# GpSimd's share of the square roots: one cubic step per piece, and 60 pieces in place of 16

## The reference

```
d2   = maximum(q2[..., :, None] + k2[..., None, :] - 2.0 * qk, 1e-12)
attn = softmax(-sqrt(d2), axis=-1)
out  = einsum('bhij,bhjd->bhid', attn, v)
```

## Time and profile before

| | us |
|---|---|
| median of 3 runs | 1478.41 |
| lowest and highest | 1476.91, 1479.61 |
| span of the profiled execution (the page gives no other time of it) | 1475.7 |
| ScalarE busy | 1445.4 |
| VectorE busy | 1245.1 |
| TensorE busy | 1125.2 |
| GpSimd busy | 632.5 |
| ScalarE's chain, share of the span | 72% |

### The profile page before, as it was taken

How to read it: one execution, slowest core, us unless ns; L and a number is a source line. 1 busy time by engine, 2 the same in 40 slices (tenths; PEclk the granted TensorE clock), 3 DMA queues, 4 the chain that set the end, 5 groups by cost and what they waited for, 6 DMA issues and landing times.

```text
span 1475.7 us, 21637 instructions
## 1 busy us (share of the span) xinstructions
PE 1125.2 (76%) x7910; PEld 441.5 (30%) x7910; DVE 1245.1 (84%) x2236; ACT 1445.4 (98%) x796; POOL 632.5 (43%) x529
## 2 busy tenths in 40 slices
PE   5587786887887988878878774787778677776766
PEld 2122223144252441542524411232123122221212
DVE  6998887988989879789798787858898898998886
ACT  3999999999999999999999999999999999999998
POOL 5166460754509577595585820732113023022100
PEclk8599998999999999999999997899999999999999
DMA  4843544213242212122121321034033033021020
GB/s 124 247 137 74 160 128 124 58 52 85 79 136 65 56 43 58 38 56 64 31 66 48 84 68 31 20 108 93 28 117 76 31 110 82 27 106 34 22 72 19
DMA packets 104061, 112.73 MB, mean 76 GB/s; under 512 B 41722, under 2 KB 76026, under 8 KB 103946
## 3 DMA queue, kind: packets, MB, share of 16 engines
q1 hardware_dynamic: 98618, 99.47, 24.5%
q0 software_dynamic: 4464, 11.09, 2.7%
q10 hardware_dynamic: 864, 0.69, 0.2%
HBM read 66.52 MB, written 44.70 MB: 75 GB/s over the span
## 4 chain that ended last, share of the span: by engine, by line
ACT 72%; issue 12%; DVE 11%; PE 3%; POOL 2%; DMA 1%; SPq 0%; ACTq 0%; DVEq 0%; POOLq 0%
ACT scores L785 28%; ACT scores L746 25%; ACT exp L1304 11%; DVE exp L1312 5%; DVE scores L695 4%; ACT exp L1300 2%; ACT ht L1037 1%; ACT L785 1%; ACT L746 1%; POOL yro L1091 1%; PE pvb L676 1%; PE ring L661 1%; ACT scores L778 0%; PE ring L1279 0%; POOL at L1254 0%
## 5 line engine op out<-in xcount | busy, mean ns | idle before, releaser
L695 DVE TENSOR_SCALAR scores<-ring 128x1024 f32<-128x1024 f32 x512 | 589.7, 1216 | 28.7 <-PE ring L661 23.5
L785 ACT ACTIVATE scores<-scores 128x8192 f32<-128x8192 f32 x63 | 438.9, 7020 | 0.2
L1304 ACT ACTIVATE exp<-ring 128x1024 f32<-128x1024 f32 x438 | 432.7, 1419 | 0.2
L746 ACT ACTIVATE scores<-scores 128x8192 f32<-128x8192 f32 (+1 forms) x59 | 404.2, 6919 | 0.2
L1279 PE MATMUL ring<-stk 128*128 128x512 bf16 x1024 | 306.7, 385 | 122.8 <-ACT exp L1304 100.1
L676 PE MATMUL pvb<-scores,val 128*9 128x256 f32 x4096 | 324.6, 392 | 80.6 <-issue 38.4
L1312 DVE SCALAR_TENSOR_TENSOR exp<-exp 128x512 f32<-128x512 f32 x438 | 322.6, 758 | 62.2 <-ACT exp L1304 56.3
L661 PE MATMUL ring<-stk 64*128 64x512 bf16 x1024 | 210.4, 408 | 56.6 <-DVE scores L695 44.5
L1279 PEld LDWEIGHTS ring<-stk 128*128 128x128 bf16 x1024 | 65.8, 97 | 338.3 <-ACT exp L1304 234.4
L661 PEld LDWEIGHTS ring<-stk 64*128 64x128 bf16 x1024 | 49.9, 93 | 288.5 <-DVE scores L695 201.8
L676 PEld LDWEIGHTS pvb<-scores,val 128*9 128x9 f32 x4096 | 65.6, 89 | 210.8 <-issue 207.4
(11 more groups left out here) (263 smaller groups left out, 1415.8 us busy)
## 6 DMA issues: line engine op xcount, KB each, us to landing
stk<-stack SPq DMA_DIRECT2D x192, 192.0 KB, 2.8
stack<-qp SPq DMA_DIRECT2D x7, 768.0 KB, 4.7
stack<-kp SPq DMA_DIRECT2D x7, 768.0 KB, 5.7
xj<-xg SPq DMA_DIRECT2D x10, 448.0 KB
yg<-xj POOLq DMA_DIRECT2D x10, 448.0 KB
stack<-qp SPq DMA_DIRECT2D x7, 512.0 KB, 5.1
stack<-kp SPq DMA_DIRECT2D x7, 512.0 KB, 5.1
stk<-sum_rows SPq DMA_DIRECT2D x128, 24.0 KB
```

Of the source, the lines that this page charges most:

```text
L695: nc.vector.tensor_scalar(S[place][:, j * N:(j + 1) * N], tile, 1e-12, None, ALU.max).then_inc(o.release(("qk", group, place, j)), 1)
L746: nc.scalar.activation(part, part, ACT.Sqrt).then_inc(root_done, 1)
L785: nc.scalar.activation(S[place][:], S[place][:], ACT.Exp, scale=-1.0).then_inc(exp_done, 1)
L1304: nc.scalar.activation(EX[k // 2][:, k % 2, :], tile, ACT.Exp, scale=SCALE1).then_inc(o.release(("qk1", n, i)), 1)
```

## The change

The pieces are laid down in a table by round and place; its entries add up to 60. A piece's root is a guess by an integer operation (with another constant) and one cubic step, nine instructions, five of them with two tensors. Rounds 1 to 15 all have pieces, at places 1, 2 and 3. ScalarE's root of a place begins behind them, and the exponential waits for the count of steps up to this place, `newton_steps`, instead of `newton_done`. In GpSimd's queue the pieces stand at several points: in round 1 ahead of the splitting of the sums, in round 2 behind it, in round 5 between the scatters, else place 1 and the first piece of place 2 ahead of the store of the attention output, the second of place 2 behind it, and place 3 at the round's end. In round 14 the deviation for layer 1 (`pool_deviation`) is moved ahead of the second piece of place 2.

```
+PIECES = [(0, 0, 0, 0), (0, 2, 0, 0), (0, 2, 1, 0), (0, 2, 2, 1), (0, 2, 0, 0), (0, 2, 0, 0), (0, 2, 2, 0), (0, 2, 2, 1),
+          (0, 2, 2, 1), (0, 2, 2, 1), (0, 2, 2, 1), (0, 2, 2, 1), (0, 2, 2, 1), (0, 2, 2, 1), (0, 2, 2, 0), (0, 2, 1, 0)]
+SEED_BITS, PIECE_STEPS = 1597063174.0, 9
+CUBIC = (-0.79078409, 1.35723565 ** 2, -2.3850909, -0.38283558)
...
-            for i in range(2):
-                x = S[NEWTON_PLACE][:, i * NEWTON:(i + 1) * NEWTON]
-                chain.step(nc.gpsimd.tensor_scalar(y.bitcast(I32), x.bitcast(I32), -0.5, NEWTON_BITS, ALU.mult, ALU.add))
+            for i in range(lo, hi):
+                o.emptied(pool, ("qk", group, place, ((i + 1) * NEWTON - 1) // N))
+                x = S[place][:, i * NEWTON:(i + 1) * NEWTON]
+                chain.step(nc.gpsimd.tensor_scalar(y.bitcast(I32), x.bitcast(I32), -0.5, SEED_BITS, ALU.mult, ALU.add))
                 chain.wait()
-                for _ in range(3):
-                    chain.step(nc.gpsimd.tensor_tensor(h, x, y, ALU.mult))
-                    chain.step(nc.gpsimd.tensor_tensor(h, h, y, ALU.mult))
-                    chain.step(nc.gpsimd.tensor_scalar(h, h, -0.5, 1.5, ALU.mult, ALU.add))
-                    chain.step(nc.gpsimd.tensor_tensor(y, y, h, ALU.mult))
-                root = nc.gpsimd.tensor_tensor(x, x, y, ALU.mult)
+                chain.step(nc.gpsimd.tensor_tensor(x, x, y, ALU.mult))
+                chain.step(nc.gpsimd.tensor_tensor(y, x, y, ALU.mult))
+                chain.step(nc.gpsimd.tensor_scalar(h, y, CUBIC[0], 1.0, ALU.add, ALU.mult))
+                chain.step(nc.gpsimd.tensor_scalar(y, y, CUBIC[2], CUBIC[3], ALU.add, ALU.mult))
+                chain.step(nc.gpsimd.tensor_tensor(h, h, h, ALU.mult))
+                chain.step(nc.gpsimd.tensor_scalar(h, h, CUBIC[1], 1.0, ALU.add, ALU.mult))
+                chain.step(nc.gpsimd.tensor_tensor(h, h, y, ALU.mult))
+                chain.step(nc.gpsimd.tensor_tensor(x, x, h, ALU.mult))
...
-            part = S[place][:, 2 * NEWTON if by_newton(group, place) else 0:CH * N]
+            part = S[place][:, pieces(group, place) * NEWTON:CH * N]
...
-            if by_newton(group, place):
-                act.wait_ge(newton_done, NEWTON_ROUNDS.index(group) + 1)
+            if pieces(group, place):
+                act.wait_ge(newton_steps, PIECE_STEPS * pieces_before(group, place + 1))
...
+                        if r == 1:
+                            pool_roots(pool, o, roots, r, 1, 0, 2)
                         pool_sums0(pool, o, chain, r)
+                    if r == 2:
+                        pool_roots(pool, o, roots, r, 1, 0, 2)
                     if FIRST_JOBS < r <= LAST_JOBS + 1:
                         pool_hidden(pool, r - 1)
-                    if r in NEWTON_ROUNDS:
-                        pool_roots(pool, o, roots, r)
...
+                    if r >= FIRST_JOBS and r != PLACE_ROUND + 1:
+                        pool_roots(pool, o, roots, r, 1, 0, pieces(r, 1))
+                        pool_roots(pool, o, roots, r, 2, 0, min(1, pieces(r, 2)))
                     if r:
                         pool_store_out(pool, r - 1)
...
+                    if r == ADD1_ROUND:
+                        pool_deviation(pool, 0, var1, std1)
+                    pool_roots(pool, o, roots, r, 2, min(1, pieces(r, 2)) if r > 2 else 0, pieces(r, 2))
                     if FIRST_JOBS < r <= LAST_JOBS + 1:
                         pool_store_jobs(pool, o, r - 1)
...
-                    if r == ADD1_ROUND:
-                        pool_deviation(pool, 0, var1, std1)
+                    pool_roots(pool, o, roots, r, 3, 0, pieces(r, 3))
```

More of the change, by code:

```diff
@@ L103, with pieces, pieces_before @@
 AUX = 3
-NEWTON, NEWTON_PLACE = 448, 1
-NEWTON_ROUNDS = [7, 8, 9, 10, 11, 12, 13, 15]
-NEWTON_BITS = 1597463174.0
+NEWTON = 448
+PIECES = [(0, 0, 0, 0), (0, 2, 0, 0), (0, 2, 1, 0), (0, 2, 2, 1), (0, 2, 0, 0), (0, 2, 0, 0), (0, 2, 2, 0), (0, 2, 2, 1), (0, 2, 2, 1), (0, 2, 2, 1), (0, 2, 2, 1), (0, 2, 2, 1), (0, 2, 2, 1), (0, 2, 2, 1), (0, 2, 2, 0), (0, 2, 1, 0)]
+SEED_BITS, PIECE_STEPS = 1597063174.0, 9
+CUBIC = (-0.79078409, 1.35723565 ** 2, -2.3850909, -0.38283558)
+def pieces(group, place):
+    return PIECES[group][place]
+def pieces_before(group, place):
+    return sum(map(sum, PIECES[:group])) + sum(PIECES[group][:place])
 PACKS = {
@@ L308, in build @@
         half_rooted = sem("half_rooted")
-        newton_steps, newton_done = sem("newton_steps"), sem("newton_done")
+        newton_steps = sem("newton_steps")
         q_stored, k_stored, sum_stored, v_stored = (
@@ L716, in pool_store_out, with pool_roots @@
                 pool.dma_start(dst, attg[:, 4 * t:4 * t + 4, :]).then_inc(att_out, 16)
[L718 to L722, removed]
+        def pool_roots(pool, o, chain, group, place, lo, hi):
             y, h = root_y[:], root_h[:]
-            for i in range(2):
-                x = S[NEWTON_PLACE][:, i * NEWTON:(i + 1) * NEWTON]
-                chain.step(nc.gpsimd.tensor_scalar(y.bitcast(I32), x.bitcast(I32), -0.5, NEWTON_BITS, ALU.mult, ALU.add))
+            for i in range(lo, hi):
+                o.emptied(pool, ("qk", group, place, ((i + 1) * NEWTON - 1) // N))
+                x = S[place][:, i * NEWTON:(i + 1) * NEWTON]
+                chain.step(nc.gpsimd.tensor_scalar(y.bitcast(I32), x.bitcast(I32), -0.5, SEED_BITS, ALU.mult, ALU.add))
@@ L727, in pool_roots @@
                 chain.wait()
-                for _ in range(3):
-                    chain.step(nc.gpsimd.tensor_tensor(h, x, y, ALU.mult))
-                    chain.wait()
-                    chain.step(nc.gpsimd.tensor_tensor(h, h, y, ALU.mult))
-                    chain.wait()
-                    chain.step(nc.gpsimd.tensor_scalar(h, h, -0.5, 1.5, ALU.mult, ALU.add))
-                    chain.wait()
-                    chain.step(nc.gpsimd.tensor_tensor(y, y, h, ALU.mult))
-                    chain.wait()
@@ L737, in pool_roots @@
-                root = nc.gpsimd.tensor_tensor(x, x, y, ALU.mult)
[L738 to L741, removed]
+                chain.step(nc.gpsimd.tensor_tensor(x, x, y, ALU.mult))
+                chain.wait()
+                chain.step(nc.gpsimd.tensor_tensor(y, x, y, ALU.mult))
+                chain.wait()
+                chain.step(nc.gpsimd.tensor_scalar(h, y, CUBIC[0], 1.0, ALU.add, ALU.mult))
@@ L2060, in fast @@
                         for place in range(1, GROUP - 1):
+                            pool_roots(pool, o, roots, r, 1, place - 1, place)
                             pool.wait_ge(att_ready, GROUP * (r - 1) + place + 1)
                             pool_scatter(pool, 2 + place)
-                    if r == PLACE_ROUND + 2:
+                    elif r == PLACE_ROUND + 2:
                         pool_scatter(pool, 7)
+                    if r >= FIRST_JOBS and r != PLACE_ROUND + 1:
+                        pool_roots(pool, o, roots, r, 1, 0, pieces(r, 1))
+                        pool_roots(pool, o, roots, r, 2, 0, min(1, pieces(r, 2)))
                     if r:
```

## The result

| kernel | median us | lowest to highest | ratio to before, 95% interval |
|---|---|---|---|
| before | 1477.66 | 1476.62 to 1479.61 (4 runs) | |
| after | 1468.36 | 1466.35 to 1469.70 (4 runs) | 0.9934 [0.9922, 0.9947] |

The change makes the kernel 9.3 us faster, 0.66%. The forecast was 1472.0 us, 6.4 us faster; its range, 1466 to 1478, held the time, but the forecast lay 3.6 us too high.

The account below looks back on a forecast made before the run. ScalarE bounds the kernel, VectorE close behind. Of at most 16.4 us, leads of 9.3 + 2.4 = 11.7, less 5.0 for collisions and 0.3 for the deviation, leave 6.4: span 1469.3, plus 2.7 gives 1472.0 us; range 1466 to 1478.

Parts of the forecast that it names:

- VectorE enters round 3 early: Rounds 1 and 2: five pieces spare ScalarE 1.86 us, and idle VectorE starts round 3 that much earlier.
- collisions at the choice, round 3: VectorE's small SBUF routing operations in round 3 wait for GpSimd's steps: 5.0 us lost, bounds 0 and 8.
- idle time picked up, rounds 4 to 13: VectorE regains the idle time ScalarE causes before rounds 9 to 13: 2.8 us.
- room at the fourth root of round 13: In round 13 VectorE's last copy ends 4.7 us before the root needing it, adding 4.7 to ScalarE's lead.
- from there to the end of round 15: Pieces of rounds 13 to 15 and round 14's wait give 2.4 us; GpSimd's earlier deviation costs 0.3.
- The mechanism: VectorE's chain decides from round 3 to 13; ScalarE pauses before round 4's fourth root, then slightly in rounds 8 to 13.
- The prediction's two parts: Round 3's routing: 2.4 us lost up to the choice, then about 3.4 on tiny operations after the ranking's 0.72.
- The piece: One GpSimd piece after the change: five tensor_tensor and four tensor_scalar steps, 8.7 us.
- Round 14: TensorE's pause vanishes and its clock takes the higher level; otherwise ScalarE stops 2.2 us.
- Rival (b): Round 14's normalisation, eight operations, also collides with GpSimd, 7.1 us against about 1.2 of room: 1477.1 us; chance 0.20.
- Rival (c): GpSimd's round becomes the bound in rounds 7 to 13, from 9.1 us per piece; about 1531 at 11 us; chance 0.09.
- The distance from the profile to the median: Median of three runs before, 1478.4 us, lay 2.7 above the profiled span; kept for the forecast.

Follow-up runs that it names:

- 60 Newton pieces: Changed kernel's 60 pieces, but with the old guess and three Newton steps instead of the cubic step: 1790.15 us (one run).
- both: Changed kernel with VectorE's choice moved ahead of the gate and up copies and round 3's last two pieces left out: 1461.51 us, 0.9898 of before.
- the first "no piece": Changed kernel without the last two pieces of round 3, beside VectorE's choice, first of two timings: 1466.02 us, 0.9930 of before.
- the four traces above: Traces of the changed kernel's three timings (1468.36, 1465.81, 1469.35 us) and of it with the deviation at its old place (1467.91 us).

## Why the prediction was right, and what it missed

The sum, step by step, as leads over the trace before:

| step | forecast | measured |
|---|---|---|
| VectorE enters round 3 early | +1.86 | +1.58 |
| collisions at the choice, round 3 | -5.0 | -1.98 (1.58 to -0.40) |
| idle time picked up, rounds 4 to 13 | +2.8 | +2.43 (-0.40 to 2.03) |
| room at the fourth root of round 13 | +4.7 | +4.70 (2.03 to 6.73) |
| from there to the end of round 15 | +2.4 - 0.3 | +2.35 (6.73 to 9.08) |
| layer 1 | 0 | +0.4 (9.08 to 9.5) |
| sum | 6.4 | 9.5 |

- **The mechanism was right.** ScalarE stops at the fourth root of round 4, then has small pauses from round 9 to 13 (the forecast said 8 to 13), and no more behind. Ten fewer pieces do not change the median by more than its spread, a shorter round 3 of VectorE does: its chain decides up to round 4, and from there to round 13 in some executions more than in others.
- **The mis-sized term is the collisions at the choice**: 5.0 us against 2.0 to 2.3, and that is nearly all of the miss. Up to L861 the three operations that were held lost 0.45 + 0.18 + 0.61 = 1.24 us, where I had 2.4. Of the five to six tiny ones that I had a step's rest each, only two were held (1.12 and 1.11 us against 0.17 and 0.18: 1.88 us, not 4 to 4.4), for by the third the pieces had ended. I had them end at 258. A piece is 8.4 us and not 8.7, and there are five in that round, which makes 1.5 us: 256.5. Sum 3.1, less the ranking's 0.72: 2.4. The prediction's two parts, 2.4 and about 3.4, come to 5.8, from which it took 5.0; so both the price of the larger ones and the number of the tiny ones were too high. And the 2.0 is not all collision: without the pieces VectorE's round 3 is 0.7 to 2.2 us shorter in the traces, no more.
- **The piece** was 0.3 us too long because I priced all five products at 1.14. The square of `root_h` has one tensor for both inputs and takes 0.93.
- **Round 14.** The clock stayed at its higher level, 1.00 in the window where it had been 0.50, so the term stands. Rival (b)'s mechanism happened: the normalisation took 6.07 us instead of 2.14, and one residual sum 5.15 instead of 2.18, 6.9 us together. It cost nothing at the end: VectorE's last copy of round 15 ends at 938.72 + 2.35 = 941.07, and the root that needs it starts at 922.13 + 26.67 - 7.02 = 941.78, 0.7 us of room left. My price of the normalisation, 7.1 us, was 3.9; and the room for it was 4.6 us, the 3.9 and the 0.7 left, where I had about 1.2. VectorE reached the deviation's wait 6.8 us early (894.72, before 901.47), for the idle times ahead of its copies of round 14, 4.63 us and then 2.5, were gone.
- **The idle time picked up** is 2.43 us as forecast, 2.8, but not from the same rounds: 0.69 from round 4 to 8, where the forecast had none, and 1.74 from 8 to 13. Why, was not traced.
- **Rival (c)** was weighed rightly: GpSimd's round 9 is 57.1 us (forecast 57.5), and it waits 1.80 us for the next tanh, at 615.64. That it would be the bound at a longer piece is shown at 14.8 us by the 60 Newton pieces, which also bear out its sum for the round; the point from which it decides was not tried.
- **Right by luck.** The lead into round 3 came out near its forecast by other ways. ScalarE's roots of round 1 started at 98.16 us and not at 99.06, so 0.90 us of lead was there before any piece. And ScalarE waited 1.71 us at round 2's fourth root, which I did not have. TensorE's granted clock was 0.52, about its 1.2 GHz level, from 124 to 129 us, where it made projections of round 1 (before: 1.00), and VectorE's chain with it was late. In the traces of both and of the first "no piece" the clock is 1.00 there, and round 2's roots have no wait.
- **The distance from the profile to the median** was taken as 2.7 us. It is 1468.36 - 1466.2 = 2.2 here; with the 3.1 of the sum these 0.5 make the 3.6 us of the miss.

## What to carry to other kernels

Work taken from the busiest engine is worth only the room that the next chain leaves: list that room place by place, and look first for what shortens the second chain (here the order of thirteen small operations, 3.1 us, where ten pieces fewer cost nothing that the timing shows). Before work goes to an idle GpSimd, look for small SBUF-to-SBUF operations of VectorE beside it on a tight stretch, and move one or the other. To price such collisions, first work out when GpSimd's run of steps ends, and count only the operations ahead of that: here two tiny ones, and not five or six.

## What the runs showed of the hardware

- **Who is held by GpSimd.** Beside the pieces a tensor_scalar of 32 columns took 1.12 us instead of 0.17, one of 224 columns 0.72 instead of 0.27, a tensor_tensor 1.00 instead of 0.39, eight tensor_scalars of 128 columns 6.07 instead of 2.15, eight scalar_tensor_tensors 5.15 instead of 2.18. The reciprocal (1.55), the reduction (0.39) and the copies from PSUM (1.22) were as long as alone. The Trainium skill, "SBUF — State Buffer", section "Who interferes with whom", says that two SBUF inputs or a two-port mode contend, and that a reduction never does; the rows agree. It also lets tensor_scalar enter such a mode; the normalisation, which I had held to be too slow for it, was held by GpSimd all the same. In which mode it ran no trace shows.
- **The price of a collision.** The two tiny operations ended when the GpSimd step beside them did: at 255.33 and 256.54, the steps at 255.28 and 256.51. They had started 0.26 and 0.06 us behind the step's start and so lost 0.95 and 0.93 us, nearly a whole step of 1.14. The eight normalisations lost 3.9 us, 0.49 each, and GpSimd's step beside them was 1.23 us instead of 1.14; another, beside a tensor_tensor that came first, took 1.33. The same section says that whoever issues first has the shared ports for its whole instruction and the other is blocked; the rows agree, as the later one waits for what is left of the earlier.
- **A product of a tensor with itself** takes GpSimd 0.932 us over 448 columns, with two different tensors 1.141.
- **The run-to-run spread** of the changed kernel is 5.5 us over 14 runs. In the traces TensorE's level differs between executions at the same place (0.50 against 1.00 ahead of round 6), and where VectorE's chain decides, such a place can reach the end: the four traces above differ in span by 3.0 us, and without ScalarE's waits of rounds 9 to 13 by 0.6.
